# A two-layer sequence model: the norm and a sum of the projection moved between engines, and attention's loads, fills, value copies and averaging rounds put in another order

## The chip, the cores and the metric

The kernel runs on one core of one Trainium2 chip (trn2). The metric is the device time of an execution in microseconds (us). Engines are called by their names: TensorE (PE in the profile, PEld for its weight loads), VectorE (DVE), ScalarE (ACT), GpSimd (POOL) and SyncE (SP), which here only issues transfers.

## The reference, cut to what matters

An input x of 4 batches x 1024 tokens x 256 channels goes through four blocks, each of them x = x + f(layernorm(x)): a state-space layer, a mixture of 8 experts, causal attention with 16 heads of 16 channels and rotated queries and keys, and a mixture of 16 experts with a shared one. The change touches the attention block alone:

```python
Q, K, V = jnp.split(jnp.einsum('bsi,oi->bso', x, W_qkv), 3, axis=-1)
Q, K, V = (to_heads(Q), to_heads(K), to_heads(V))
Q, K = (apply_rope(Q), apply_rope(K))        # x0*cos - x1*sin, x0*sin + x1*cos
scores = jnp.einsum('bhqd,bhkd->bhqk', Q, K) / jnp.sqrt(jnp.float32(d_k))
scores = jnp.where(causal, scores, -jnp.inf)
attn = jax.nn.softmax(scores, axis=-1)
out = jnp.einsum('bhqk,bhkd->bhqd', attn, V)
```

## The kernel before, in words

The program is a chain of phases (front, run_experts, project_qkv, attention, back, run_experts, finish), each in a block of its own: no engine begins a phase before all have ended the one ahead. Inside a phase each engine has its own queue, written out in full and executed in order, and the queues meet only at semaphores. Two phases matter.

**project_qkv** (line 1222) takes the 4096 tokens in 8 groups of 512, four tiles of 128 each. GpSimd gathers the rows of two experts for each token by indirect transfers (line 1337, eight a group). VectorE's add_experts (from line 1373) multiplies them by their weights and adds them to x in two rounds of four instructions (lines 1379 and 1383), then takes mean and variance and writes var_eps (line 1392). GpSimd raises it to the power -1/2 (line 1343), VectorE's normalise writes the normed rows (line 1398, two pointers: mean and factor), TensorE transposes them (line 1479), ScalarE copies the result (line 1441), and TensorE multiplies it by the weights: four products for queries and keys, even and odd channels apart (line 1490), and one for the values (line 1497), which ScalarE copies (line 1448). Rotation is four products of VectorE for queries and four for keys (rotate, line 1406) and then, on GpSimd, a difference and a sum for each (add_turned, lines 1350 and 1351). ScalarE rounds each result (hi, line 1454), VectorE takes what is left (lo, line 1411), and SyncE stores both parts to DRAM, eight transfers a group. The loops run over ticks; in a tick each engine works on different groups:

```python
for tick in range(groups + 2):                     # GpSimd, line 1354
    gather(tick + 1, first half); rsqrt(tick); gather(tick + 1, second half)
    add_turned(tick - 2, 0); add_turned(tick - 2, 1)
```

VectorE's order in a tick is add_experts(tick), four differences of tick - 3, normalise(tick), rotate(tick - 1); ScalarE's is copy_xn(tick), four roundings of tick - 2, copy_v(tick). SyncE stores in its tick the sum x2 of the group, the values of the group before and the queries and keys of the group three back, and waits in that order.

**attention** (line 1508) takes 32 pairs of heads (eight a batch), numbered p. For a pair it needs queries and keys in both parts, spread over partitions 0 to 63 (load, line 1624, eight transfers of 128 KB, each into 16 partitions, all on SyncE's queue), in a ring of four places (RINGQ). Partitions 64 up hold fills: zeros in qs, ones in ks; the row at partition 96 of qs is the negated maximum of each query, which a transfer puts there (row, line 1638). Two passes over the scores follow. In the first, TensorE computes 24 pieces of up to 512 keys (piece, line 1781) and VectorE takes the running maximum of each (line 1724). The pieces go through a ring of four PSUM banks; after the last, TensorE transposes the maxima into the next bank of that same ring (transpose_max, line 1787) and ScalarE negates them (negate, line 1736), which frees the bank. In the second pass TensorE computes the transposed scores in 18 chunks (line 1795) and ScalarE takes their exponentials (line 1743); GpSimd masks the 16 diagonal squares (line 1698). Then TensorE averages the values in ten rounds, four products side by side in each (average, line 1811), the profile counting each of them as two; round 8 and 9 with 128 columns, the others with 256. The values of a batch come in one transfer of 1 MB (load_v, line 1636) and GpSimd copies them to place (values, line 1690, eight copies).

All engines follow one count of steps, 18 a pair (NX): at step 18p + i TensorE issues chunk j of an earlier pair, whose second pass begins LAG = 27 steps after its first (so j = i + 9 modulo 18, of pair p - 2 up to i = 8 and of pair p - 1 from i = 9 on), at i = TURN = 2 the transposed maxima of pair p - 1, then one or two pieces of pair p, and then rounds of the averages, where avg_at names j. ScalarE in a step runs the exponential of that chunk, then at i = 3 negate(p - 1), in this order:

```python
avg_at = {1: (0, 1), 5: (2, 3), 9: (4, 5), 12: (6, 7), 16: (8, 9)}     # line 1587
```

With j = i + 9 the five blocks stand at i = 10, 14, 0, 3 and 7. The piece in slot x waits for the release of what lay four places earlier in the ring (bank_free, line 1766): for x = 5, issued at i = 4, that is the bank of the transposed maxima. The steps i = 0 and 1 issue x = 0 and 1, i = 2 issues x = 2 and 3, i = 3 issues x = 4.

SyncE's loop (line 1652) issues per tick load(tick + 1), load_v at each eighth tick, a store and row(tick - 1); load(p) waits until the chunks of pair p - 4 are done. At the start it issues load(0), load(1), the values, load(2), then row(0), and load(3) ahead of row(1). Four fills come first: GpSimd's zeros (line 1677, 64 x 8192), later and vs (lines 1679 and 1680), VectorE's ones (line 1711, 64 x 8192). TensorE runs keep_busy products (line 1818) meanwhile and waits for all fills; where no chunk is due it runs keep_busy in the chunk's place. At step 72 ScalarE issues the fetch of 4 MB of expert weights (line 2446).

## Time and profile before

| | us |
|---|---|
| median of 3 runs | 1811.72 (1811.04 to 1818.42) |
| the profiled execution | 1815.95 |
| its span in the trace | 1814.2 |
| TensorE busy | 1567.3 (86%) |
| VectorE busy | 1014.3 (56%) |
| ScalarE busy | 707.6 (39%) |
| GpSimd busy | 565.3 (31%) |

The trace is that of the profiled execution, counted from its span's start; project_qkv lies between about 751 and 925 us, attention between 925 and 1440. TensorE's matmuls are pipelined and their ends modelled, so that its rows overlap. A row "x4" joins four instructions: its us is from the first's start to the last's end. What stands in brackets at the end of a row is how long the engine was idle before it and what released it. PEclk is TensorE's granted clock as a share of 2.4 GHz: 0.50 is the lower level, 1.2 GHz.

### The profile page before, as it was taken

To read this page: it belongs to the slowest core of one execution; us is meant where nothing else is said; L and a number is where in the kernel's file an instruction comes from. 1 tells how busy PE (TensorE), PEld (TensorE's weight loads), DVE (VectorE), ACT (ScalarE), POOL (GpSimd) and SP (SyncE) were. 2 spreads that over 40 slices of the span, in tenths; PEclk is the share of its full clock that TensorE was granted. 3 is DMA by queue.
4 is the path that set the end of the run, shared out by engine and by line. 5 is a ranking of instruction groups with operands and counts; after the bars stand their busy time and mean duration, and the time that the engine had idled before them with its cause. 6 is when DMAs were issued, how large, how long until landed. Compare 5 with 4: busy or idle time off the path is not lost. (4 is left out here: it accounts for less than half of the span.)

```text
span 1814.2 us, 29698 instructions
## 1 busy us (share of the span) xinstructions
PE 1567.3 (86%) x9335; PEld 1107.4 (61%) x9335; DVE 1014.3 (56%) x3338; ACT 707.6 (39%) x1487; POOL 565.3 (31%) x993
## 2 busy tenths in 40 slices
PE   0999999982999999588658999999999668399998
PEld 0577777771666666454336666666666456288787
DVE  1245444442222222378858778878888257465556
ACT  0444444430222222122205667767777512154410
POOL 2122333344000000378522232232332238500076
PEclk9899999995999999799779999999999867599999
DMA  8100111112222221358596866666764276445444
GB/s 296 54 24 25 47 47 47 36 53 96 67 65 65 65 66 57 122 177 288 178 199 79 173 108 94 93 102 95 116 91 72 63 228 209 177 153 157 136 134 147
DMA packets 150807, 204.08 MB, mean 112 GB/s; under 512 B 20352, under 2 KB 119168, under 8 KB 150400
## 3 DMA queue, kind: packets, MB, share of 16 engines
q1 hardware_dynamic: 102688, 130.05, 32.1%
q10 hardware_dynamic: 35680, 38.56, 6.2%
q0 software_dynamic: 12288, 33.57, 5.7%
q8 instruction: 80, 1.31, 0.3%
q14 instruction: 71, 0.58, 0.1%
HBM read 116.91 MB, written 84.93 MB: 111 GB/s over the span
## 5 line engine op out<-in xcount | busy, mean ns | idle before, releaser
L1743 ACT ACTIVATE t_probs<-t_ps_st 128x512 f32<-128x512 f32 x576 | 313.7, 596 | 145.5 <-PE t_ps_st L1795 138.5
L1724 DVE CUSTOM_DVE_ANT_0 t_seen<-t_ps_s,t_later 128x512 bf16<-128x512 f32 (+3 forms) x512 | 286.2, 587 | 25.2 <-PE t_ps_s L1781 22.9
L1795 PE MATMUL t_ps_st<-t_qs,t_ks 128*128 128x512 f32 (+3 forms) x768 | 247.0, 371 | 10.0 <-DMA t_qs<-t_neg_max 7.6
L1781 PE MATMUL t_ps_s<-t_ks,t_qs 96*128 96x512 f32 (+3 forms) x768 | 251.9, 369 | 0.5 <-ACT t_neg_max L1736 0.5
L1698 POOL TENSOR_SCALAR_AFFINE_SELECT t_probs<-t_probs 128x128 f32<-128x128 f32 x512 | 136.4, 304 | 297.2 <-ACT t_probs L1743 295.5
L1795 PEld LDWEIGHTS t_ps_st<-t_qs,t_ks 128*128 128x128 f32 x768 | 139.6, 193 | 86.0 <-ACT t_probs L1743 37.8
L1724 DVE CUSTOM_DVE_ANT_0 t_seen<-t_ps_s,t_later,t_first_max 128x512 bf16<-128x512 f32 (+3 forms) x256 | 140.6, 549 | 57.5 <-PE t_ps_s L1781 57.3
L1337 POOL DMA_INDIRECT d_ye<-outputs_dram,r_pos_all x64 | 64.1, 1002 | 326.8 <-POOLq L1099 309.0
L1811 PE MATMUL t_ps_o<-t_probs,t_vs 128*17 128x256 f32 (+1 forms) x2560 | 157.0, 364 | 3.3 <-POOL t_probs L1698 2.8
L1781 PEld LDWEIGHTS t_ps_s<-t_ks,t_qs 96*128 96x128 f32 x768 | 142.5, 195 | 17.2 <-ACT t_neg_max L1736 0.8
L832 PE MATMUL ps_h<-w_in,xnt 128*128 128x512 f32 x256 | 125.5, 615 | 23.1 <-ACT xnt L666 23.1
L1131 PE MATMUL m_ps_h<-w_sb,m_xt 128*128 x284 | 135.5, 600 | 0.0
L1146 PE MATMUL m_ps_y<-w_sb,m_ht 128*128 x568 | 134.2, 379 | 0.0
L1202 ACT ACTIVATE m_xt<-m_ps_x 128x256 f32<-128x256 f32 x150 | 57.5, 383 | 174.5 <-PE m_ps_x L1124 174.5
L1174 DVE TENSOR_TENSOR m_h<-m_ps_h,b_sb 128x512 f32<-128x512 f32 x71 | 49.1, 692 | 131.6 <-PE m_ps_h L1131 129.7
L2223 POOL DMA_INDIRECT f_ye<-outputs_dram,r_pos_all x64 | 62.9, 983 | 170.1 <-POOLq L1099 151.0
L1212 ACT ACTIVATE m_ht<-m_ps_ht 128x128 f32<-128x128 f32 (+1 forms) x150 | 63.9, 426 | 128.2 <-PE m_ps_ht L1139 128.0
L1146 PEld LDWEIGHTS m_ps_y<-w_sb,m_ht 128*128 128x128 f32 x568 | 102.5, 190 | 11.0
L1811 PEld LDWEIGHTS t_ps_o<-t_probs,t_vs 128*17 128x17 f32 x2560 | 59.5, 97 | 75.4 <-issue 27.1
L1124 PE MATMUL m_ps_x<-ident,m_x_t 128*128 128x128 f32 x300 | 58.7, 278 | 41.5 <-DMA m_x_t<-gathered_dram 40.3
L351 POOL TENSOR_TENSOR xi<-xi,sig_z 128x512 f32<-128x512 f32 x32 | 40.6, 1269 | 161.1 <-ACT sig_z L678 160.9
L1185 DVE TENSOR_TENSOR m_y<-m_ps_y,b_sb 128x256 f32<-128x256 f32 x71 | 30.1, 424 | 104.7 <-PE m_ps_y L1146 104.7
(306 smaller groups left out, 2797.9 us busy)
## 6 DMA issues: line engine op xcount, KB each, us to landing
m_x_t<-gathered_dram SPq DMA_DIRECT2D x150, 128.0 KB, 2.1
outputs_dram<-m_y ACTq DMA_DIRECT2D x150, 128.0 KB, 1.7
t_qs<-qkt_dram SPq DMA_DIRECT2D x128, 128.0 KB, 5.8
t_ks<-qkt_dram SPq DMA_DIRECT2D x128, 128.0 KB, 5.9
qkt_dram<-d_hi SPq DMA_DIRECT2D x32, 256.0 KB, 4.1
qkt_dram<-d_lo SPq DMA_DIRECT2D x32, 256.0 KB, 4.1
headst_dram<-t_att SPq DMA_DIRECT2D x32, 256.0 KB, 7.3
x_t<-in_x_dram SPq DMA_DIRECT2D x8, 512.0 KB, 4.4
```

The lines of the kernel that those rows point to most:

```text
L832: last = nc.tensor.matmul(ps_h[h][:], xnt[:, n % 2, j, :], w_in[:, j, h * DI:(h + 1) * DI], start=(j == 0), stop=(j == KD - 1))
L1131: last = nc.tensor.matmul(ps_h[t % 2][:], xt[:, t % 2, j, :], w_up[:, j, bass.ts(expert[t], width)], start=(j == 0), stop=(j == KD - 1))
L1146: last = nc.tensor.matmul(ps_y[t % 2][:], ht[:, t % 2, j, :], w_down[:, j, bass.ts(expert[t], DM)], start=(j == 0), stop=(j == blocks - 1))
L1212: nc.scalar.activation(ht[:, t % 2], ps_ht[t % 2][:], ACT.Relu if relu else ACT.Copy).then_inc(ht_ready, 1)
L1337: nc.gpsimd.indirect_dma_start(out=ye[:, g % 2, j, i, :], out_offset=None, in_=outputs[:, :], in_offset=bass.IndirectOffsetOnAxis(ap=kept[ ...
L1698: nc.gpsimd.affine_select(out=diag, in_=diag, compare_op=ALU.is_ge, fill=0.0, base=0, pattern=[[1, P]], channel_multiplier=-1).then_inc(ma ...
L1724: nc.vector.tensor_tensor_reduce(out=seen[:, (NP * p + x) % (RS + 1), 0:keys], in0=bank_of(p, x)[:, 0:keys], in1=masks, scale=1.0, scalar= ...
L1743: nc.scalar.activation(probs[:, p % 2, i // NST, base:base + STC], ps_st[(NX * p + i) % RT][:], ACT.Exp, scale=HD ** -0.5).then_inc(exp_re ...
L1781: nc.tensor.matmul(bank_of(p, x)[:, 0:keys], qs[0:MAX_ROW, at, qc * P:(qc + 1) * P], ks[0:MAX_ROW, at, k0:k0 + keys], start=True, stop=Tru ...
L1795: last = nc.tensor.matmul(ps_st[(NX * p + i) % RT][:, col:col + width], ks[:, at, kc * P:(kc + 1) * P], qs[:, at, q0:q0 + width], start=Tr ...
L1811: last = nc.tensor.matmul(ps_o[32 * g:32 * g + VR, col:col + width], vs[:, (p // PAIRS) % 2, kc, 2 * (p % PAIRS) + head, :], probs[:, p % ...
L2223: nc.gpsimd.indirect_dma_start(out=ye[:, g % R, j, i, :], out_offset=None, in_=outputs[:, :], in_offset=bass.IndirectOffsetOnAxis(ap=kept[ ...
```

## The change

In project_qkv the norm is written by ScalarE from a bias (-mean times factor), which VectorE computes in a new small instruction (shift); GpSimd's power waits until the norm before it has read its factor. Of the four results of the rotation, the last sum goes from GpSimd to VectorE (last_sum), with a semaphore of its own. ScalarE's order in a tick is normalise(tick), copy_v(tick - 1), copy_xn(tick), the roundings.

In attention the fills are cut by ring place: place 0 first (VectorE fills its ones), the others on GpSimd after the mask table; TensorE waits for three small fills and, at a pair's first piece, for its place. The keys of pair 0 are loaded on ScalarE's queue. SyncE issues load(0), load(1), then row(0), then load(2) and the first values, then load(3) ahead of row(1). The values of a later batch are loaded at tick 4 of the batch before and copied at its tick 5, after that tick's masks. The rounds stand in four blocks: by j = i + 9 at i = 11, 16, 2 and 7.

```diff
+            def shift(g):
                 dve.wait_ge(rstd_ready, g + 1)
-                wait(dve, xnt_done, KD * g)
-                for j in range(J):
-                    nc.vector.tensor_scalar(xn[:, j, :], x2[:, g % 2, j, :], mean_var[:, j, 0:1], rstd[:, j:j + 1],
-                                            ALU.subtract, ALU.mult).then_inc(xn_ready, 1)
+                wait(dve, xn_ready, J * g)
+                nc.vector.scalar_tensor_tensor(out=bias[:], in0=mean_var[:, :, 0], scalar=-1.0, in1=rstd[:], op0=ALU.mult,
+                                               op1=ALU.mult).then_inc(bias_ready, 1)
+
+            def last_sum(g):
+                dve.wait_ge(by_ready, 8 * g + 8)
+                wait(dve, lo_ready, NB * g)
+                nc.vector.tensor_tensor(qk[:, NB - 1, :], by[:, g % 2, 1, 2, :], by[:, g % 2, 1, 3, :], ALU.add).then_inc(last_sum_ready, 1)
...
                 if live(tick):
-                    normalise(tick)
+                    shift(tick)
+                if live(tick - 2):
+                    last_sum(tick - 2)
...
+            def normalise(g):
+                act.wait_ge(bias_ready, g + 1)
+                wait(act, xnt_done, KD * g)
+                for j in range(J):
+                    nc.scalar.activation(xn[:, j, :], x2[:, g % 2, j, :], ACT.Identity, bias=bias[:, j:j + 1],
+                                         scale=rstd[:, j:j + 1]).then_inc(xn_ready, 1)
...
-    avg_at = {1: (0, 1), 5: (2, 3), 9: (4, 5), 12: (6, 7), 16: (8, 9)}
+    avg_at = {2: (0, 1, 2), 7: (3, 4), 11: (5, 6, 7), 16: (8, 9)}
...
             load(0)
-            for tick in range(pairs + 5):
-                if live(tick + 1):
+            load(1)
+            for tick in range(1, pairs + 5):
+                if tick > 1 and live(tick + 1):
                     load(tick + 1)
-                if live(tick) and tick % PAIRS == 0:
-                    load_v(tick // PAIRS)
+                if tick % PAIRS == PAIRS // 2 and live(tick + PAIRS // 2):
+                    load_v(tick // PAIRS + 1)
                 if live(tick - 4):
                     store(tick - 4)
                 if live(tick - 1):
                     row(tick - 1)
+                if tick == 1:
+                    load(2)
+                    load_v(0)
...
-            nc.gpsimd.memset(qs[KS:P].bitcast(FP32), 0.0).then_inc(q_zeroed, 1)
...
+            zero_rows(0)
...
+            for p in range(1, RINGQ):
+                zero_rows(p)
+                nc.gpsimd.memset(ks[KS:P, 2 * p:2 * p + 2].bitcast(FP32), 1.0).then_inc(rows_filled, 1)
...
+                if tick == 0:
+                    values(0)
                 if live(tick - 2):
                     mask(tick - 2)
+                if tick % PAIRS == PAIRS // 2 + 1 and live(tick + PAIRS // 2):
+                    values(tick // PAIRS + 1)
...
-            nc.vector.memset(ks[KS:P].bitcast(FP32), 1.0).then_inc(filled, 1)
+            nc.vector.memset(ks[KS:P, 0:2].bitcast(FP32), 1.0).then_inc(filled, 1)
...
+            for part in range(4):
+                load_rows(act, 0, ks, 1, part, part // 2)
...
-            pe.wait_ge(filled, 5)
-            pe.wait_ge(q_zeroed, 1)
+            pe.wait_ge(filled, 3)
```

## Rows read from the trace of the kernel before

**Rows 1.** Stretches: us, busy time by engine (x count), PEclk, DMA share, GB/s
```profile
1216.69:1231.17 14.48, 14.48 (x137) 9.46 (x133) 12.51 (x49) 10.41 (x21) 4.29 (x16) 1.00 0.67 93
...
952.36:971.48 19.12, 14.69 (x57) 11.75 (x56) 13.84 (x51) 7.60 (x14) 4.73 (x16) 0.82 0.63 73
...
971.48:985.01 13.53, 13.23 (x108) 8.87 (x112) 12.18 (x49) 9.90 (x21) 4.23 (x16) 1.00 0.62 80
...
1062.71:1080.65 17.94, 16.35 (x137) 10.41 (x133) 12.78 (x49) 10.58 (x22) 9.17 (x33) 0.90 0.70 131
...
1182.19:1202.17 19.98, 17.67 (x137) 10.99 (x133) 12.93 (x49) 10.70 (x21) 9.16 (x33) 0.83 0.65 120
...
1303.71:1319.30 15.59, 14.60 (x137) 9.55 (x133) 12.53 (x49) 10.43 (x22) 9.13 (x33) 1.00 0.79 146
...
961.00:967.00 6.00, 6.00 (x17) 5.03 (x18) 4.14 (x15) 3.66 (x7) 0.58 (x2) 0.50 0.49 57
...
925.00:936.80 11.80, 8.14 (x14) 3.49 (x15) 7.45 (x3) 0.00 (x0) 11.49 (x4) 0.79 0.95 118
```

**Rows 2.** Timeline of GpSimd, project phase: start us, us, instruction
```profile
854.12 1.27 POOL L1351 TENSOR_TENSOR d_qk<-d_by 128x512 f32<-128x512 f32 x1
...
860.54 1.22 POOL L1343 TENSOR_TENSOR d_rstd<-d_var_eps,mhalf 128x4 f32<-128x4 f32 x1
```

**Rows 3.** Timeline of VectorE, project phase
```profile
854.15 2.72 DVE L1379 SCALAR_TENSOR_TENSOR d_part<-d_ye,r_prob_all,d_x 128x256 f32<-128x256 f32 x4 [1.66 <-issue]
...
856.79 1.67 DVE L1383 SCALAR_TENSOR_TENSOR d_x<-d_ye,r_prob_all,d_part 128x256 f32<-128x256 f32 x4
...
860.09 0.17 DVE L1392 TENSOR_SCALAR d_var_eps<-d_mean_var 128x4 f32<-128x4 f32 x1
...
876.40 0.17 DVE L1392 TENSOR_SCALAR d_var_eps<-d_mean_var 128x4 f32<-128x4 f32 x1
...
876.48 3.56 DVE L1411 TENSOR_TENSOR d_lo<-d_qk,d_hi 128x512 f32<-128x512 f32 x4
...
879.96 4.21 DVE L1398 TENSOR_SCALAR d_xn<-d_x,d_mean_var,d_rstd 128x256 f32<-128x256 f32 x4
```

**Rows 4.** Instructions of line 2120: duration ns min/median/max, first and last start
```profile
L2120 ACT ACTIVATE k_xn<-whole_sum,k_bias,k_rstd x32: 583/588/601, 1459.1 to 1557.3; 128x256 f32<-128x256 f32 x32
```

**Rows 5.** Timeline of ScalarE, end of the project phase
```profile
900.08 0.60 ACT L1448 ACTIVATE d_v<-d_ps_v 128x512 f32<-128x512 f32 x1 [1.13 <-PE d_ps_v L1497]
```

**Rows 6.** Timeline of TensorE, start of attention
```profile
936.42 0.94 PE L1818 MATMUL t_ps_st<-causal,ident 128*128 128x256 f32 x2 [3.53 <-POOL t_vs L1680]
...
960.86 0.80 PE L1795 MATMUL t_ps_st<-t_qs,t_ks 128*128 128x512 f32 x1 [4.14 <-DMA t_qs<-t_neg_max]
...
974.20 0.45 PE L1795 MATMUL t_ps_st<-t_qs,t_ks 128*128 128x512 f32 x1
```

**Rows 7.** DMA issues at 952.7 and 1055.5: KB each, us to landing
```profile
t_qs<-t_neg_max SPq DMA_DIRECT2D x1, 8.0 KB, 8.1
...
t_v_raw<-v_dram SPq DMA_DIRECT2D x1, 1024.0 KB, 10.8
```

**Rows 8.** Timeline of TensorE, quiet pair, steps i = 3 and 4
```profile
1230.69 1.06 PE L1811 MATMUL t_ps_o<-t_probs,t_vs 128*17 128x256 f32 x16
...
1231.68 0.50 PE L1795 MATMUL t_ps_st<-t_qs,t_ks 128*128 128x512 f32 x1
...
1232.02 0.34 PE L1781 MATMUL t_ps_s<-t_ks,t_qs 96*128 96x384 f32 x1
```

**Rows 9.** Timeline of ScalarE, the same stretch
```profile
1231.17 0.25 ACT L1736 ACTIVATE t_neg_max<-t_ps_s 16x128 fp32r<-16x128 f32 x1
...
1232.21 2.15 ACT L1743 ACTIVATE t_probs<-t_ps_st 128x512 f32<-128x512 f32 x4 [0.79 <-PE t_ps_st L1795]
```

**Rows 10.** Timeline of TensorE's weight loads, pair 2
```profile
970.21 0.19 PEld L1781 LDWEIGHTS t_ps_s<-t_ks,t_qs 96*128 96x128 f32 x1 [0.33 <-DVE t_first_max L1724]
...
971.78 0.19 PEld L1781 LDWEIGHTS t_ps_s<-t_ks,t_qs 96*128 96x128 f32 x1 [0.80 <-ACT t_neg_max L1736]
```

More of the change, by code:

```diff
@@ L1254, in project_qkv @@
     rstd = sb("d_rstd", [P, J])
+    bias = sb("d_bias", [P, J])
     xn = sb("d_xn", [P, J, DM])
@@ L1461, in _ @@
                         round_qk(tick - 2, n)
-                if live(tick):
-                    copy_v(tick)
         @block.tensor
```

66 lines of the change are left out of this document (42 added, 24 removed).

## The prediction, made before the changed kernel ran

> **What bounds the kernel now.** I read the busy time by stage first. In a quiet pair of the attention phase [rows 1], between two negations, TensorE is busy for all 14.48 us at the full 2.4 GHz, VectorE 12.51, ScalarE 10.41, GpSimd 4.29: there TensorE sets the pace, and any wait that is put into its queue lengthens the pair. The same view shows where pairs are longer: 19.12 us for the first, at a mean granted clock of 0.82, and 17.94, 19.98 and 15.59 us where a batch begins.
>
> The project phase is read on GpSimd's and VectorE's rows [rows 2, 3]. One variance follows the other by 16.31 us (860.09, 876.40). The ring behind that: four gathers on GpSimd, their landing, add_experts on VectorE, the power on GpSimd, four gathers. GpSimd has no gap in it: eight gathers, four sums 1.24 us apart (850.42 to 855.39, of which the row is the last), four gathers, the power at 860.54. VectorE's first part of add_experts starts at 854.15 and takes 2.72 us for four, ending at 856.87, that is 1.48 after GpSimd's last sum.
>
> **The change, part by part. Project phase.** (a) One of GpSimd's four sums goes to VectorE: GpSimd's way to the next power is 1.24 us shorter. VectorE's way is not, fully: the gathers end where the sums begin, 850.42, and add_experts starts 3.73 later, when they have landed; its second four, which nothing slows, take 1.67 us (856.79 [rows 3]), so the first four end at 855.82 instead of 856.87 at best. I take 0.9 us a turn, between 0.6 and 1.24, for the five turns that have sums (groups 3 to 7): -4.6 us. (b) The norm goes from VectorE to ScalarE. In most turns this is beside other work. In the last it is on the path: GpSimd's sums run beside VectorE there, the differences take 3.56 us and the norm 4.21 (879.96 to 884.17) [rows 3]. On ScalarE the same form (128x256, two pointers) takes 588 ns [rows 4], four in 2.2 us, starting after the differences at 880.0 and ending at 882.3. After it stands the copy of the values of the group before (1.1 us), which was ahead of it. The moved sum on VectorE is then ahead of the rotation: 0.7 us alone, up to 1.75 beside GpSimd's sums. Gain 2.1 us (bounds 0.5 and 3). The small product for the bias and the added waits (power after norm, product after norm) find their signals given some 10 us earlier: nothing. From the last values (900.08 [rows 5]) SyncE issues 24 transfers and sets the end; that tail is as before, only earlier. Sum: -6.7 us (-9 to -3).
>
> The row is that three instructions with two SBUF inputs or a doubled rate (first part, difference, norm) stretch beside GpSimd's sums [rows 3]. The Trainium skill (SBUF — State Buffer, "Who interferes with whom") says that a VectorE instruction with two SBUF inputs contends with a GpSimd one that reads SBUF; the moved sum is such a one. By it the sum would cost a full GpSimd sum more in the last turn, and the term would be 1 us smaller.
>
> **Start of attention.** Before, TensorE waited until 936.42 for the fills [rows 6]; the phase starts at 925. The fills by ring place free it at about 929, but the first megabyte of queries and keys moved at 118 GB/s with the queues already at a busy share of 0.95 [rows 1], so it needs 8.9 us after some 2 of latency: 936.3. Gain 0.4 us. Bounds: nothing, and 3.5 us (keep_busy ends at 932.9) if keys on ScalarE's queue doubled the rate.
>
> The Trainium skill (SBUF — State Buffer, "Can I just issue two DMAs to hit both halves?") gives +6% for two transfers at once; by it the gain would be 0.9 us. No run here shows it yet.
>
> Then the queue of SyncE. Before, the row of pair 0 stood behind load(1), the values and load(2) and took 8.1 us to land [rows 7]; TensorE idled 4.14 us before the first chunk [rows 6] and then ran 6 us at 1.2 GHz (granted 0.50) [rows 1]. After, that row goes out alone: both are gone. But load(2), the values and load(3) are now issued behind it, from 952.9 on. A load takes 11 us from its first issue (8.9 and 2) and 8.9 behind another, the values land some 3.6 after the load ahead of them (10.8 from their own issue [rows 7], 7.2 of it behind the load): 963.9, 967.5, 976.4. TensorE is at the first chunk at 956.3 (960.86 - 4.14 - 0.4) and nine steps on, at VectorE's 12.51 / 18 = 0.7 us, it wants load(2) for pair 2: 962.6, so it waits to 964. The row of pair 1 is issued three steps later, some 966.5, **behind load(3)**, and lands at 976.5; six steps after its issue, at 971, it is needed. So chunk (1, 0), at 974.20 before [rows 6], comes at 976.5: 2.3 us later; and a wait of 5 us is followed by 6 us at half clock as the first one was, 3 us more. Start in all: +5.3 us by the third negation (-7 to +8: the lower end is both old losses gone and no new one).
>
> **Beginning of a batch.** The three cost 3.46 + 5.50 + 1.11 = 10.1 us over 14.48 [rows 1], from the row behind load and values, the masks behind the value copies on GpSimd, and the clock after both. The masks' part goes: in mid-batch the copies (2.8 us) stand between two pairs' masks. The row's part moves along to pairs 3, 11 and 19, since load_v still stands behind a load and ahead of a row. At pair 3 it meets the 4 MB of weights that ScalarE fetches at step 72; I give it 4 us there and 0.5 at each of the others. Term: -5.0 us (-9 to -1).
>
> **Blocks of averages.** Around a block TensorE holds the next chunk for 0.34 us (1231.68 to 1232.02) instead of 0.24, and the piece ahead of the block loses as much: 0.2 us a block [rows 8]. One fewer in 31 pairs: -6.2 us. But what stood in the removed places matters. The ring has four banks for the pieces, and the transposed maxima take one; the piece at i = 4 (x = 5) reuses it and waits for negate. ScalarE runs negate after the exponential of chunk i = 3. Before, a block stood at i = 3 between the two: negate ran from 1231.17 to 1231.42 [rows 9], the piece came at 1232.02 [rows 8], 0.6 us to spare. After, the block (three rounds) is at i = 2, ahead of chunk i = 3. From that chunk's start: 0.50 for the chunk [rows 8], 0.03, 0.53 for the exponential (2.15 for four [rows 9]), 0.25, 0.05 make 1.36 us; TensorE gets to the piece after 0.34 + 0.12 + 0.24 = 0.70. **A new wait of 0.66 us in 29 pairs** (3 to 31): +19.1 us. The trace has one pair without a block there, pair 2: its weight load waited 0.80 us for that negation (971.78), and the one before waited 0.33 for the maximum that frees a bank (970.21) [rows 10]. For this second wait, and one for the last maximum (the block at i = 0 covered both; now it is at i = 16), I take 0.25 us a pair, between nothing and 0.37: +7.3 us. Term: +20.2 us (+10 to +24).
>
> **Sum:** -6.7 + 5.3 - 5.0 + 20.2 = +13.8 us. The profiled execution took 1815.95 us (span 1814.2), 4.2 above the median of the three runs, 1811.72; so 1829.8 for such an execution and **1825.5 us** for the median. A measurement of this kernel can tell about 0.5% (9 us) from no change.
>
> **Rivals.** (A) The new wait is not paid. If negate came in time, or TensorE had room that its modelled ends hide, the blocks give -6.2 alone: -6.7 + 5.3 - 5.0 - 6.2 = -12.6, 1799 us, faster. For it: no wait of TensorE is recorded in quiet pairs. Against it: pair 2, and 14.48 of 14.48 busy. It decides where ScalarE's negation ends less than 0.70 us after chunk i = 3 starts; an exponential and the negation alone are 0.78. (B) The loads at the start drain in time: if load(3) lands before 971 no row waits, the start is -7 instead of +5.3, and the whole is +1.5: 1813 us. It needs 3.1 MB in the 16 us to 971, near 200 GB/s; the rows give 118 for query and key loads, and 146 where values are among them (1303.71 [rows 1]). (C) The three waits within 2 us let the clock fall in each pair: 14.48 us has then some 3 us at half rate, +1.5 us in 29 pairs, 1869 us. Against it: the 13.53 us after pair 2's waits were granted 1.00 [rows 1].
>
> **How the numbers follow.** My forecast has 0.55 (0.48 of it above +9 us), A 0.20, B 0.17, C 0.08. Slower by over 0.5%: 0.48 + 0.08 = 0.56; within: 0.07 + 0.17 = 0.24; faster: 0.20. The likeliest case alone spans 1817 to 1836 (its terms' ends, seldom all together). The range goes down to 1797, which takes in most of A, and up to 1836; C and the tail of A are left out.
>
> **What would show it.** Each step right: variances 15.4 us apart in the project phase and the last value copy some 6.7 us earlier; first chunk without a wait; a wait of some 5 us at chunk (1, 0) named by the transfer of the negated maxima; no masks awaited at a batch's beginning; quiet pairs of 15.1 to 15.2 us, with TensorE waiting for t_neg_max at line 1781's matmul in nearly every pair. Quiet pairs of 14.3 us would make A right and the forecast wrong; a third negation before 978 (by the old phase's start) would make B right.

## The result, and the profile after

The changed kernel takes 1827.44 us (median of 7 runs, 1824.85 to 1829.17), the kernel before 1812.86 on the same chip (median of 7, 1809.52 to 1819.13): a ratio of 1.0079, with a 95% interval of 1.0063 to 1.0094. It is 14.6 us slower; 1825.5 us was forecast. The profiled execution has a span of 1825.5 us against 1814.2, 11.3 more.

How the 11.3 us come about can be read from marks in the two traces: the first variance of the project phase, SyncE's first load of the attention phase, the third negation, and the last negation (pair 31).

| from ... to ... | before | after | difference |
|---|---|---|---|
| start, first variance (nothing changed there) | 768.4 | 766.3 | -2.1 |
| first variance, first load of attention | 156.7 | 148.3 | -8.4 |
| first load, third negation | 59.9 | 67.2 | +7.3 |
| third negation, last negation | 435.4 | 448.5 | +13.1 |
| last negation, end | 393.8 | 395.1 | +1.3 |

The project phase gave more than forecast, the start of attention took more, and the long middle of attention lost what the blocks of averages cost, less what the beginnings of batches gave.

**Project phase.** VectorE's and then ScalarE's timeline of the changed kernel:

```profile
766.31 0.17 DVE L1396 TENSOR_SCALAR d_var_eps<-d_mean_var 128x4 f32<-128x4 f32 x1
...
869.69 0.17 DVE L1396 TENSOR_SCALAR d_var_eps<-d_mean_var 128x4 f32<-128x4 f32 x1
...
873.25 1.22 DVE L1401 SCALAR_TENSOR_TENSOR d_bias<-d_mean_var,d_rstd 128x4 f32<-128x4 f32 x1
874.40 0.68 DVE L1407 TENSOR_TENSOR d_qk<-d_by 128x512 f32<-128x512 f32 x1
```

```profile
874.51 2.07 ACT L1453 ACTIVATE d_xn<-d_x,d_bias,d_rstd 128x256 f32<-128x256 f32 x4 [8.34 <-DVE d_bias L1401]
...
889.82 0.60 ACT L1467 ACTIVATE d_v<-d_ps_v 128x512 f32<-128x512 f32 x1 [1.13 <-PE d_ps_v L1521]
```

The eight variances span 103.38 us (766.31 to 869.69); before it was 107.98 (768.42 to 876.40). In the late turns one follows the other by 15.17 to 15.29 us, where it was 16.31. From the last variance to the last copy of values it is 20.13 us, and was 23.68 [rows 3, 5]. The bias, a 128x4 instruction, takes 1.22 us in the last turn, since GpSimd's sums run beside it; in the turn before it takes 0.15. Even so the norm is done at 876.58, 6.89 us after the variance, where it was 7.77.

**Quiet pairs.** The stretches between negations in the changed kernel (columns as in [rows 1]); 958.81 to 981.83 is pair 2, the line below it the 6 us behind its wait, 1095.28 to 1110.50 a quiet pair, the last two are pairs 12 and 20, in which the values of the next batch travel:

```profile
942.71:958.81 16.10, 13.84 (x57) 10.10 (x56) 13.49 (x53) 7.45 (x14) 0.37 (x2) 0.89 0.93 150
958.81:981.83 23.02, 16.38 (x114) 10.54 (x113) 12.97 (x52) 9.93 (x20) 8.89 (x33) 0.85 0.70 79
967.96:973.96 6.00, 6.00 (x35) 3.68 (x36) 2.49 (x9) 2.09 (x4) 0.29 (x1) 0.63 1.03 117
981.83:1001.54 19.71, 15.24 (x129) 10.07 (x129) 12.39 (x49) 10.14 (x22) 4.34 (x16) 0.95 0.83 171
1001.54:1019.17 17.63, 17.16 (x130) 11.26 (x129) 12.76 (x50) 10.48 (x21) 4.38 (x16) 0.86 1.08 249
1095.28:1110.50 15.22, 14.73 (x129) 9.72 (x129) 12.48 (x50) 10.23 (x21) 4.34 (x16) 1.00 0.64 88
1125.72:1141.70 15.98, 14.95 (x129) 9.72 (x129) 12.57 (x50) 10.29 (x21) 4.34 (x16) 1.00 0.74 129
1248.35:1263.68 15.33, 14.83 (x129) 9.74 (x129) 12.49 (x50) 10.29 (x22) 4.34 (x16) 1.00 0.78 138
```

A quiet pair now takes 15.22 us, of which TensorE is busy for 14.73, at a granted clock of 1.00. Before, 14.48 of 14.48 were busy [rows 1]. The waits of TensorE between 920 and 1460 us (total, times, longest) name what is new:

```profile
PE t_ps_s L1827 <- ACT t_neg_max L1778: 13.7, 30, 0.5
PE t_ps_st L1841 <- DMA t_qs<-t_neg_max: 6.8, 2, 6.3
PE t_ps_s L1827 <- DMA t_ks<-qkt_dram: 6.6, 2, 4.4
PE t_ps_st L1841 <- ACT t_probs L1785: 5.3, 6, 4.1
PE t_ps_o L1857 <- issue: 0.5, 1, 0.5
```

The first line is a wait for the negation in 30 pairs; before there was one such wait. Masks, which had held TensorE three times at the beginnings of batches, are no longer in the list. The wait itself, in TensorE's timeline of a quiet pair:

```profile
1094.26 0.50 PE L1841 MATMUL t_ps_st<-t_qs,t_ks 128*128 128x512 f32 x1
1094.59 0.28 PE L1827 MATMUL t_ps_s<-t_ks,t_qs 96*128 96x256 f32 x1
1094.71 0.39 PE L1841 MATMUL t_ps_st<-t_qs,t_ks 128*128 128x512 f32 x1
1095.59 0.45 PE L1827 MATMUL t_ps_s<-t_ks,t_qs 96*128 96x384 f32 x1 [0.48 <-ACT t_neg_max L1778]
```

and in ScalarE's:

```profile
1094.79 0.60 ACT L1785 ACTIVATE t_probs<-t_ps_st 128x512 f32<-128x512 f32 x1 [1.99 <-PE t_ps_st L1841]
1095.28 0.25 ACT L1778 ACTIVATE t_neg_max<-t_ps_s 16x128 fp32r<-16x128 f32 x1
```

The chunk of i = 3 starts at 1094.26, its exponential at 1094.79, the negation behind it at 1095.28, and the piece that needs the bank at 1095.59. That is 1.33 us after the chunk's start; the forecast had worked out 1.36 from parts. TensorE's gap is 0.48 us.

**Start of attention.** TensorE's waits there, and how long the row of pair 1 took to land:

```profile
926.44 0.79 PE L1827 MATMUL t_ps_s<-t_ks,t_qs 96*128 96x512 f32 x1 [4.39 <-DMA t_ks<-qkt_dram]
955.13 0.59 PE L1827 MATMUL t_ps_s<-t_ks,t_qs 96*128 96x512 f32 x1 [2.21 <-DMA t_ks<-qkt_dram]
...
967.96 0.79 PE L1841 MATMUL t_ps_st<-t_qs,t_ks 128*128 128x512 f32 x1 [6.26 <-DMA t_qs<-t_neg_max]
```

```profile
t_qs<-t_neg_max SPq DMA_DIRECT2D x1, 8.0 KB, 8.8
```

The row of pair 0, issued at 943.06 on an empty queue, landed in 2.3 us, and chunk (0, 0) did not wait. The row of pair 1, issued at 959.14 behind the loads of pairs 2 and 3 and the values, took 8.8 us; chunk (1, 0) waited 6.26 us for it, and the 6 us after that had a granted clock of 0.63. Pair 3 then lost time in a way that the forecast had not spelled out. ScalarE's timeline, then TensorE's:

```profile
992.35 7.17 ACTq L2491 DMA_DIRECT2D wgu_sb<-in_w_gu_dram  x2
...
999.56 2.08 ACT L1785 ACTIVATE t_probs<-t_ps_st 128x512 f32<-128x512 f32 x4 [6.62 <-issue]
```

```profile
1000.21 0.80 PE L1841 MATMUL t_ps_st<-t_qs,t_ks 128*128 128x512 f32 x1 [4.14 <-ACT t_probs L1785]
```

ScalarE needed 7.17 us to issue two transfers of 2 MB each, its exponentials stood behind them, and TensorE waited 4.14 us for an exponential. In the kernel before the same two issues cost ScalarE 3.58 us and TensorE 1.65.

### The profile page after: what moved, and what is told of

The parts are those of the page before. It is cut to its first block and busy times, and to the rows that moved or that the text cites. A ratio compares the mean times of both kernels' runs of the same rounds, so it can differ in the third digit from the quotient of the medians.

```text
span 1825.5 us, 29737 instructions
## 1 busy us (share of the span) xinstructions
PE 1573.9 (86%) x9335; PEld 1118.3 (61%) x9335; DVE 998.3 (55%) x3322; ACT 714.3 (39%) x1519; POOL 563.8 (31%) x991
## 5 line engine op out<-in xcount | busy, mean ns | idle before, releaser
L1766 DVE CUSTOM_DVE_ANT_0 t_seen<-t_ps_s,t_later 128x512 bf16<-128x512 f32 (+3 forms) x512 | 290.5, 587 | 86.2 <-PE t_ps_s L1827 84.2
L1827 PE MATMUL t_ps_s<-t_ks,t_qs 96*128 96x512 f32 (+3 forms) x768 | 261.6, 375 | 20.8 <-ACT t_neg_max L1778 13.7
L1841 PE MATMUL t_ps_st<-t_qs,t_ks 128*128 128x512 f32 (+3 forms) x768 | 242.1, 366 | 12.3 <-DMA t_qs<-t_neg_max 6.8
L1857 PE MATMUL t_ps_o<-t_probs,t_vs 128*17 128x256 f32 (+1 forms) x2560 | 149.9, 362 | 0.5 <-issue 0.5
```

Source lines behind the costliest of these rows:

```text
L1766: nc.vector.tensor_tensor_reduce(out=seen[:, (NP * p + x) % (RS + 1), 0:keys], in0=bank_of(p, x)[:, 0:keys], in1=masks, scale=1.0, scalar= ...
L1827: nc.tensor.matmul(bank_of(p, x)[:, 0:keys], qs[0:MAX_ROW, at, qc * P:(qc + 1) * P], ks[0:MAX_ROW, at, k0:k0 + keys], start=True, stop=Tru ...
L1841: last = nc.tensor.matmul(ps_st[(NX * p + i) % RT][:, col:col + width], ks[:, at, kc * P:(kc + 1) * P], qs[:, at, q0:q0 + width], start=Tr ...
L1857: last = nc.tensor.matmul(ps_o[32 * g:32 * g + VR, col:col + width], vs[:, (p // PAIRS) % 2, kc, 2 * (p % PAIRS) + head, :], probs[:, p % ...
```

## The experiments

Twelve kernels ran, in four groups, each group on one chip. Ratios are to the kernel before on that chip (its median was 1841.77 us in the first group, 1812.86, 1813.72 and 1814.38 in the others), so it is the ratios that are compared from group to group. On the chip of the first group the extra time lies behind attention: from the last negation to the end a1_old_blocks takes 422.4 us, the changed kernel on the other chip 395.1. The table also gives, from each profile, the time from SyncE's first load to the third negation and to the last one, and a quiet pair. Each profile is of one execution, which can lie some us beside its kernel's median (8 us below it for a2_before_new_blocks, 4 above it for d3_old_order).

| kernel | ratio, 95% interval | to 3rd negation | to last | quiet pair |
|---|---|---|---|---|
| before | 1 | 59.9 | 495.3 | 14.48 |
| changed | 1.0079 [1.0063, 1.0094] | 67.2 | 515.8 | 15.22 |
| a1_old_blocks | 0.9969 [0.9949, 0.9989] | 64.1 | 493.8 | 14.49 |
| a2_before_new_blocks | 1.0097 [1.0059, 1.0134] | 57.3 | 505.1 | 15.22 |
| a3_negate_first | 0.9993 [0.9970, 1.0016] | 64.4 | 494.7 | 14.49 |
| a4_row_first | 1.0055 [1.0031, 1.0078] | 62.2 | 512.7 | 15.23 |
| b3_blocks_0_3 | 0.9959 [0.9944, 0.9973] | 66.3 | 492.7 | 14.29 |
| c1_fetch_later | 1.0066 [1.0046, 1.0086] | 67.1 | 513.8 | 15.23 |
| c2_project_alone | 0.9947 [0.9932, 0.9962] | 58.4 | 494.5 | 14.49 |
| c3_keys_on_sync | 1.0097 [1.0076, 1.0119] | 65.2 | 514.2 | 15.23 |
| d1_blocks_row | 0.9920 [0.9895, 0.9945] | 59.2 | 484.2 | 14.29 |
| d3_old_order | 0.9899 [0.9877, 0.9921] | 56.6 | 484.3 | 14.29 |
| e1_old_order_fetch | 0.9905 [0.9881, 0.9928] | 54.7 | 480.4 | 14.29 |
| f1_values_behind_row | 0.9909 [0.9888, 0.9929] | 54.5 | 477.2 | 14.29 |

### The blocks of averages

**The old blocks in the changed kernel.**

```diff
-    avg_at = {2: (0, 1, 2), 7: (3, 4), 11: (5, 6, 7), 16: (8, 9)}
+    avg_at = {1: (0, 1), 5: (2, 3), 9: (4, 5), 12: (6, 7), 16: (8, 9)}
```

> The changed kernel with the five old blocks of averages (at steps 10, 14, 0, 3 and 7 of a pair). Theory (the removed blocks had covered TensorE's waits for the maxima and the negation): the quiet pair comes back from 15.22 to about 14.48 us, no wait of TensorE for t_neg_max at line 1827's matmul is left beyond pair 2, and the kernel is some 20 us faster than the changed one, 1807 us, a ratio of 0.996 to the kernel before. Rival A (the blocks' places don't matter, each block costs 0.2 us): one block more in 31 pairs makes it 6 us slower than the changed kernel, 1834 us. If part of the slower pair comes from the other edits (order on ScalarE's or GpSimd's queue), the pair stays above 14.6 us.

Measured: a ratio of 0.9969, 0.0110 below the changed kernel's 1.0079, which is 20 us of 1812.86 (the two intervals together leave about 15 to 25). A quiet pair:

```profile
1072.43:1086.94 14.51, 14.51 (x137) 9.48 (x133) 12.51 (x49) 10.45 (x21) 4.30 (x16) 1.00 0.67 93
```

TensorE is busy throughout again. Rival A, by which it would have been slower, is out.

**The new blocks in the kernel before.** The edit of a1_old_blocks the other way round, in the kernel before.

> The kernel before with the four new blocks alone. Theory: quiet pair 15.2 us against 14.48, TensorE's waits for t_neg_max in nearly every pair, and 20 to 23 us slower than the kernel before: ratio 1.011 to 1.013. Rival A: 6 us faster, ratio 0.997. If the new places only hurt together with the other edits, the ratio is between the two.

```profile
1106.57:1121.76 15.19, 14.71 (x129) 9.71 (x129) 12.47 (x50) 10.22 (x21) 4.34 (x16) 1.00 0.63 88
```

```profile
PE t_ps_s L1781 <- ACT t_neg_max L1736: 14.4, 30, 0.6
...
PE t_ps_o L1811 <- POOL t_probs L1698: 0.9, 2, 0.6
```

The pair is 15.22 us and the wait is there 30 times: the blocks alone make it, with none of the other edits. But the ratio is 1.0097 where 1.011 to 1.013 was expected (the interval reaches both), and in the trace the attention phase is only 9.8 us longer than before, not 21. The losses at the beginnings of batches shrank: pairs 8, 9, 16 and 24 take 15.88, 15.55, 16.65 and 15.72 us, 2.9 over the quiet 15.22 together, where the kernel before lost 10.1 (and c2_project_alone, with the same attention, 11.0). In the traces, then, the parts of this change don't add: beside the new blocks the move of the values is worth some 2 us, beside the old ones 8. That a slower pair gives the masks and rows the slack that they lacked is a reading that was not tried by itself. Nor do the times show it: the profiled execution was the fastest of four, 8.3 us below their median, and the ratio stands for 18 us (11 to 25 by its interval), not for the trace's 9.8.

**The negation ahead of the exponential.**

```diff
-                if live(q):
-                    exponentials(q, j)
                 if i == 3 and live(p - 1):
                     negate(p - 1)
+                if live(q):
+                    exponentials(q, j)
```

> The changed kernel, with ScalarE's negation put ahead of the exponential of the same step. It touches one of the two waits alone: the piece that reuses the bank of the transposed maxima. Theory: this wait is the 0.66 us a pair of the forecast; the negation comes 0.5 us sooner, TensorE's wait for t_neg_max goes, and the kernel is 12 to 19 us faster than the changed one (1808 to 1815 us), the quiet pair 14.6 to 14.8 us; the waits for t_row_max and t_first_max, 0.2 to 0.3 us a pair, stay. Rival: TensorE's pace in these pairs is set by the waits for the maxima alone (they only move); then it is within 4 us of the changed kernel, with the pair still at 15.2. A second rival: the negation now waits on ScalarE for the maximum, and the exponential behind it comes late; then the pair is longer than 15.2.

```profile
1091.13:1105.62 14.49, 14.48 (x130) 9.75 (x129) 12.46 (x49) 10.01 (x21) 4.37 (x16) 1.00 0.65 93
```

Ratio 0.9993, some 16 us faster than the changed kernel. The quiet pair fell by the whole 0.73 us, more than expected, with the four blocks where they were. The wait is one of order on ScalarE's queue: an exponential of 0.6 us ahead of a negation of 0.25 that TensorE wants sooner.

**Four blocks that cover both waits.** Blocks at i = 11, 0, 3 and 7.

```diff
-    avg_at = {2: (0, 1, 2), 7: (3, 4), 11: (5, 6, 7), 16: (8, 9)}
+    avg_at = {2: (0, 1, 2), 9: (3, 4), 12: (5, 6, 7), 16: (8, 9)}
```

> The changed kernel, still with four blocks of averages, but at steps 11, 0, 3 and 7 of a pair: blocks stand again in the two places that had covered the waits (the last maximum, and the negation). Theory: no wait is left and there is one block less than before, so the quiet pair falls below the 14.48 us of the kernel before, to about 14.28 us; 25 to 29 us faster than the changed kernel, ratio to the kernel before 0.992 to 0.994. Rival: a block costs nothing by itself and the pair with all waits covered is 14.48 us, as it was with five blocks and with the negation put first; then it is 22 us faster than the changed kernel, ratio 0.996. Second rival: a block of three rounds at step 0 or 3 keeps the banks so long that another wait shows; pair above 14.6 us.

```profile
1077.88:1092.22 14.34, 14.34 (x137) 9.69 (x133) 12.42 (x49) 10.15 (x21) 4.25 (x16) 1.00 0.69 94
```

Most pairs take 14.29 us (this one 14.34). Against a1_old_blocks (14.49, five blocks, all covered) that is 0.20 us for one block; against a3_negate_first (14.49, four blocks, the negation mended, the last maximum uncovered) it is 0.20 us for the other wait. That wait shows on TensorE's weight loads in a3_negate_first, in every pair, and nowhere in b3_blocks_0_3:

```profile
1104.81 0.09 PEld L1833 LDWEIGHTS t_ps_s<-ident,t_row_max 128*16 128x16 f32 x1 [0.18 <-DVE t_row_max L1766]
...
1105.36 0.19 PEld L1827 LDWEIGHTS t_ps_s<-t_ks,t_qs 96*128 96x128 f32 x1 [0.33 <-DVE t_first_max L1766]
```

So the 0.73 us of the change are +0.73 for the negation, +0.20 for the maximum, -0.20 for the block less. The ratio, 0.9959, is a little above the 0.992 to 0.994 expected: 22 us faster than the changed kernel, not 25 to 29. Its third negation comes as late as in the changed kernel, and pair 12, where the values travel, now takes 17.96 us against 14.29: with a shorter pair its row is late again (see the last experiment).

### The start of attention

**The row of pair 1 ahead of the load of pair 3.**

```diff
+                if tick == 2:
+                    row(1)
                 if tick > 1 and live(tick + 1):
                     load(tick + 1)
...
-                if live(tick - 1):
+                if live(tick - 1) and tick != 2:
                     row(tick - 1)
```

> The changed kernel, with the row of pair 1 issued ahead of the load of pair 3 on SyncE's queue. Theory (the row lands behind the load's data): TensorE's wait of 6.26 us at chunk (1, 0) falls to under 1 us, the stretch after it is no longer at a lowered granted clock, and the kernel is 6 to 9 us faster than the changed one. The load of pair 3 is issued some 11 us later and must not be late: it is needed near 976 us. Rival: the row waits for the loads already in flight (pair 2 and the values), whatever stands behind it; then the wait stays at 5 us or more and the time is the changed kernel's. Second rival: the loss moves to pair 3 (its load or the weights that ScalarE fetches there): wait at chunk (1, 0) gone, time gained under 3 us.

The waits of TensorE between 955 and 996 us that are left:

```profile
955.40 0.50 PE L1829 MATMUL t_ps_s<-t_ks,t_qs 96*128 96x512 f32 x1 [2.21 <-DMA t_ks<-qkt_dram]
...
971.15 0.50 PE L1829 MATMUL t_ps_s<-t_ks,t_qs 96*128 96x512 f32 x1 [1.29 <-DMA t_ks<-qkt_dram]
...
995.44 0.79 PE L1843 MATMUL t_ps_st<-t_qs,t_ks 128*128 128x512 f32 x1 [4.20 <-ACT t_probs L1787]
```

The row lands in 1.8 us, the wait of 6.26 us at chunk (1, 0) is gone, and the third negation comes 5.1 us earlier. But 2 us are given back by the fifth: the load of pair 3, now behind the row, is 1.29 us late, and the wait for ScalarE's blocked queue is followed by a longer stretch at half clock. Over the 8.5 us behind that wait the granted clock is 0.50 (995.44 to 1003.94), where it is 0.62 in the changed kernel (1000.20 to 1008.70). Six of these us:

```profile
996.77:1002.77 6.00, 5.81 (x32) 4.49 (x31) 3.06 (x12) 3.62 (x8) 1.38 (x5) 0.50 1.09 346
```

The ratio is 0.0024 below the changed kernel's, 4 us; the two intervals overlap, so that the times alone would not show the gain. The trace does: 3.1 us over the phase.

**The keys of pair 0 back on SyncE's queue.**

```diff
-                    if p > 0:
-                        load_rows(sp, p, ks, 1, part, part // 2)
+                    load_rows(sp, p, ks, 1, part, part // 2)
...
-            for part in range(4):
-                load_rows(act, 0, ks, 1, part, part // 2)
```

> The changed kernel with the keys of pair 0 issued by SyncE again, not by ScalarE. Theory (the first megabyte is limited by its transfer, at 117 GB/s with the queues full): TensorE's first piece comes 11.8 us after the phase's start as with two queues, and the time is within 2 us of the changed kernel. Rival: two queues did bring something that the other fills hid; then the first piece is 1 us or more later. Second rival: the load of pair 1 no longer overtakes the keys of pair 0, so that the first piece comes earlier.

The ratio is 1.0097, with an interval that overlaps the changed kernel's: no difference that can be told, and if one, against this kernel. In the trace the first piece comes 11.06 us after the first load, not 11.83. But over the ten kernels that load with two queues it comes 10.95 to 11.83 us after (10.95 in a1_old_blocks, 11.21 in f1_values_behind_row). So one execution with one queue doesn't tell which is sooner, and the second queue brought TensorE nothing that shows.

**SyncE's old order at the start, with the mended blocks.** In b3_blocks_0_3:

```diff
             load(0)
-            load(1)
-            for tick in range(1, pairs + 5):
-                if tick > 1 and live(tick + 1):
+            for tick in range(pairs + 5):
+                if live(tick + 1):
                     load(tick + 1)
+                if tick == 0:
+                    load_v(0)
...
-                if tick == 1:
-                    load(2)
-                    load_v(0)
```

> The changed kernel with blocks at steps 11, 0, 3 and 7, and SyncE's order at the start as in the kernel before (load of pair 1, values, load of pair 2, then row 0, load of pair 3, row 1); the values of later batches stay in mid-batch. Theory: the new order at the start is a loss in itself, since it moves two megabytes of loads from before row 0 to behind it, and the queues have nothing to do before it. The third negation comes 57 to 60 us after the phase's start, as in the kernel before, not 66 to 67; ratio 0.991 to 0.993, some 5 us faster than with the mended blocks alone. Rival: the row of pair 0 now stands behind the loads and lands late again (4 us, and 3 of lowered clock), so that the kernel is no faster than with the blocks alone, ratio 0.996.

Ratio 0.9899 against 0.9959, 11 us faster than with the mended blocks alone, and the third negation comes 56.6 us after the phase's start, not 66.3. The new order of the loads was a loss in itself: its gain on row 0 (2.3 us to land, not 8.1 [rows 7]) is smaller than what it costs to hold back two megabytes of loads until the queue is wanted for the next row. The rival's wait for row 0 came back in part: 2.72 us at chunk (0, 0) in this execution, none in the two later kernels with the same start (e1_old_order_fetch and f1_values_behind_row, where that row took 3.9 and 3.0 us to land).

**Both mendings, with the new order.** The diffs of b3_blocks_0_3 and a4_row_first together.

> The changed kernel with both mendings: blocks at steps 11, 0, 3 and 7, and the row of pair 1 issued ahead of the load of pair 3. Theory (the two losses are in different pairs and add): ratio 0.9959 of the blocks alone, less the 0.0024 that the row's place gave, makes 0.9935. In the trace the third negation comes some 62 us after the phase's start (67.2 in the changed kernel) and half of the 5 us is lost again at pairs 3 and 4. Rival: with shorter pairs nothing of the row's gain is left by pair 5, because the transfers of the start, 4 MB of weights among them, set the time; ratio 0.996.

Ratio 0.9920, 7 us below b3_blocks_0_3; the phase is 8.4 us shorter (484.22 against 492.65), where the row's place alone gave 3.1 in the changed kernel. The third negation comes at 59.2, sooner than the 62 expected, and pairs 3 and 4 give nothing back (36.2 us against 36.1). The rival is out. So of the 9.8 us by which the old order is ahead at the third negation, moving one row gives back 7.1. This kernel and d3_old_order are equal over the attention phase; whether the 0.0021 between their ratios is real can't be told, since their intervals overlap.

### The fetch and the values

**The fetch of weights in pair 6**, in the changed kernel.

```diff
-                if step == 4 * NX:
+                if step == 6 * NX + 9:
                     fetch(act)
```

> The changed kernel, with the two fetches of weights on ScalarE's queue (4 MB) issued at step 117 (in pair 6) and not at step 72 (pair 4). Theory: ScalarE's 6.62 us of issue come from a transfer queue that is full at that time (load of pair 5, values and stores stand there too), and TensorE's 4.14 us for t_probs follow from it; later, with the values out of the way, the issue takes 3.6 us or less and TensorE waits under 2 us: 2 to 5 us faster than the changed kernel, with pairs 3 and 4 together below 33 us instead of 37.3. Rival: the issue of 4 MB takes 6.6 us wherever it stands; the loss moves to pair 6 unchanged, time within 1.5 us.

Pairs 3 and 4 come down to 15.22 us each. The two issues now take ScalarE 2.86 us (1030.80 to 1033.66) and not 7.17, and no wait of TensorE for an exponential is over 0.3 us. But the 4 MB still have to travel. TensorE's wait and the stretch behind it, in pair 7:

```profile
1049.71 0.50 PE L1841 MATMUL t_ps_st<-t_qs,t_ks 128*128 128x512 f32 x1 [2.76 <-DMA t_qs<-t_neg_max]
```

```profile
1043.35:1050.00 6.65, 3.59 (x31) 2.78 (x32) 3.76 (x16) 3.50 (x8) 1.89 (x7) 1.00 1.07 307
1050.00:1056.00 6.00, 6.00 (x39) 3.42 (x39) 3.06 (x11) 2.61 (x6) 0.29 (x1) 0.72 1.12 204
```

Now a row stands behind the weights, and the pair takes 19.77 us. Of 6.9 us at pairs 3 and 4, 5.2 are lost at pairs 6 and 7. The ratio is 1.0066, 2 us better, which the intervals can't tell from nothing. The same edit in d3_old_order:

> The same as the one before, and the fetch of weights at step 117. Theory: pair 3 or 4 no longer waits for ScalarE's blocked queue; the 4 MB take transfer time from one pair later on, 4.5 us there against 6.9 at pairs 3 and 4: 2 us faster than without, ratio 0.990 to 0.992. Rival: with the old order the loads of the start have drained by pair 4 (the kernel before lost 5.2 us at pairs 3 to 5), and the later fetch gains nothing, within 1 us.

Ratio 0.9905 against 0.9899: no difference. The phase is 3.9 us shorter in the trace (480.4 against 484.3), the whole is not measurably so. And the 3.9 are not the fetch's: pairs 3 and 4 take 6.8 us less than in d3_old_order, pairs 6 and 7 6.5 more; the rest is the first pairs and pair 12, which the fetch doesn't touch.

**The project phase alone**, in the kernel before (the functions of that phase from the changed kernel, nothing else):

> The kernel before with the project phase of the changed one alone (the sum on VectorE, the norm on ScalarE). Theory: the whole gain of that phase reaches the end: 6.7 us by the forecast, 8.2 by the two traces, so a ratio of 0.995 to 0.996. Rival: the phase is shorter but the attention phase that follows starts with transfers still under way and loses part of it: 0.998. Quiet pairs of 14.48 us.

Ratio 0.9947, 9.6 us faster (interval 6.9 to 12.3). The whole gain of the phase reaches the end; the attention phase behind it takes 494.5 us, as before. The rival is out.

**The values of mid-batch behind the row.** In d3_old_order the pair with the values takes 19.67 us. Its window, TensorE's wait in it, and the landing of that row:

```profile
1112.52:1132.19 19.67, 17.43 (x137) 11.06 (x133) 12.68 (x49) 10.40 (x21) 4.27 (x16) 0.83 0.69 131
```

```profile
1119.24 0.80 PE L1839 MATMUL t_ps_st<-t_qs,t_ks 128*128 128x512 f32 x1 [2.23 <-DMA t_qs<-t_neg_max]
```

```profile
t_qs<-t_neg_max SPq DMA_DIRECT2D x1, 8.0 KB, 6.4
```

```diff
-                if tick % PAIRS == PAIRS // 2 and live(tick + PAIRS // 2):
-                    load_v(tick // PAIRS + 1)
                 if live(tick - 4):
                     store(tick - 4)
                 if live(tick - 1):
                     row(tick - 1)
+                if tick % PAIRS == PAIRS // 2 and live(tick + PAIRS // 2):
+                    load_v(tick // PAIRS + 1)
```

> The kernel with mended blocks and the old order at the start, and in mid-batch the values issued behind the row of tick 4, not ahead of it (the load of the next pair is issued some 3.5 us later). In the run without this, pair 12 takes 19.67 us against 14.29: a wait of 2.23 us for the row, which took twice as long to land as in a quiet pair, and a granted clock of 0.83 after it; pairs 4 and 20 have smaller losses. Theory (the row lands late because one megabyte of values is ahead of it): pairs 12 and 20 come down to 14.3 to 15 us, 5 us less in all, ratio 0.987. Rival: the load of the next pair meets the values and lands late, so that the loss moves one pair on; ratio 0.990 as without it.

```profile
1105.85:1120.13 14.28, 14.28 (x137) 9.67 (x133) 12.39 (x49) 10.11 (x21) 4.25 (x16) 1.00 0.88 163
1002.24:1019.99 17.75, 16.09 (x137) 10.05 (x133) 12.49 (x49) 10.18 (x22) 6.96 (x24) 0.90 0.75 113
```

Pair 12 is quiet, as is pair 20 (14.29): the row had been late because a megabyte of values was ahead of it. But pair 5 (the second line) takes 17.75 us, where it took 14.40 in d3_old_order. In this execution the values issued at 987.29, behind the weights (979.24), took 13.1 us to land, and the row of pair 4, issued at 1002.51, took 5.8; TensorE waited 1.66 us for it. For that batch the loss moved one pair on, as the rival says, though by the row and not by the load. Those were the values of the second batch; the ones of the third and fourth, at pairs 12 and 20, meet no weights. The phase is 7.1 us shorter (477.2 against 484.3), but the ratio is 0.9909 against 0.9899: the theory holds for its pairs and fails in its time. Whether the 7 us exist outside the profiled execution stays open; the first pairs of attention differ by some us from one execution to the next (the kernel before and c2_project_alone run the same attention phase, and their first chunk waited 4.14 and 3.02 us), and this profiled execution lies 5.7 us below its kernel's median, that of d3_old_order 3.9 above.

The best kernels of the study are d3_old_order, e1_old_order_fetch, f1_values_behind_row and d1_blocks_row, at 0.990 to 0.992 of the kernel before (15 to 18 us faster, and faster than both kernels of the comparison). Nothing measured here tells the four apart.

## Why the prediction was right

The forecast was +13.8 us, the measurement +14.6 between medians and +11.3 between the two profiled spans, to which the measured column below adds up within 0.1. It came out by its main term, which has the right mechanism and size. The other terms each missed by 1.7 to 2.5 us, with signs that cancel; that the total is within 1 us of the medians is luck. The last row of the table lies in stretches that the change doesn't touch, so it is a difference between two executions.

| step | forecast | measured | from |
|---|---|---|---|
| project phase | -6.7 | -8.4 | the two traces; -9.6 by c2_project_alone |
| start, to the third negation | +5.3 | +7.3 | the two traces |
| beginnings of batches, pairs 3 to 5 | -5.0 | -7.5 | -9.2 and +1.7, below |
| blocks | +20.2 | +20.6 | what is left of the middle's +13.1 without the row above; 20 by a1_old_blocks |
| rest | 0 | +1.3 and -2.1 | behind attention, and ahead of the project phase |

**Project phase.** The turns gave 4.60 us (103.38 against 107.98), where 4.6 was forecast, but not as forecast. The step "I take 0.9 us a turn" was too small: in the late turns GpSimd waits for no other engine after the change either, and they are shorter by 1.0 to 1.1 us (15.17 to 15.29 against 16.31), nearly the 1.24 of the sum that it gave away; the five turns with sums gave 5.2. The third variance came 0.64 us later after the second than before (14.16 against 13.52), which the forecast had at nothing, and that brought the sum back to 4.60. The last turn gave 3.55 us, not 2.1. The norm ended only 0.9 us sooner after its variance than before; TensorE began its products for queries and keys 0.9 us sooner after the norm (1.59 against 2.45), and 1.8 us came from these products, which took 8.16 us and not 9.97. The windows of the kernel before and of the changed one over them show the clock at which they ran:

```profile
886.60:896.60 10.00, 9.98 (x17) 4.40 (x18) 8.31 (x12) 1.66 (x4) 5.68 (x4) 0.71 0.31 99
```

```profile
878.20:886.30 8.10, 8.10 (x17) 3.72 (x18) 8.00 (x11) 2.39 (x5) 4.91 (x3) 0.87 0.95 299
```

The forecast had left the clock out there. It had weighed a rule of the Trainium skill (SBUF — State Buffer, "Who interferes with whom") by which the moved sum, with two SBUF inputs beside GpSimd's sums, would make the term 1 us smaller. The trace agrees that the two contend, and either side can pay: in the last turn that sum took 0.68 us beside a sum of GpSimd's, which stretched to 1.80 us against 1.28 alone; in the two ticks after it, the same sum of VectorE's took 1.57 and 1.56 us beside GpSimd's. The term was larger than forecast all the same, not smaller.

**Start.** Waits were where they had been put: none at chunk (0, 0), 2.21 us for the load of pair 2 (about 1.5 forecast), 6.26 us at chunk (1, 0) for a row that stood behind the load of pair 3 (5 forecast), and a lowered clock after it. The row was wanted at 961.7 and came at 968; a4_row_first shows that the queue's order did it, since the row then lands in 1.8 us. What was missed is the first piece, which came 11.83 us after the phase's start, where it had been 11.71, and not 0.4 earlier; the first negation came 0.8 us later, which is within what executions differ by (26.5 to 28.6 us after the first load). The transfers of keys on ScalarE's queue bought nothing that shows: with one queue (c3_keys_on_sync) that piece comes at 11.06, with two at 10.95 to 11.83, the queues being at a busy share of 0.96 in c3_keys_on_sync and in the changed kernel. By the Trainium skill (SBUF — State Buffer, "Can I just issue two DMAs to hit both halves?") two transfers at once would have brought some 6%; of the 8.9 us of transfer that is an estimated 0.5 us, less than the 0.9 between these executions, so that no run here shows it. The term as a whole is more than a chance of one execution: the third negation comes 64.1 to 67.2 us after the first load in the six kernels that start as the changed one (65.7 in the mean; c3_keys_on_sync, with its keys on SyncE, is among them), and 57.3 to 59.9 in the three that start as the one before (58.5), 7.2 apart.

**Beginnings of batches.** The kernel before lost 10.1 us there. After, pairs 12 and 20 lost 0.76 and 0.11, and the masks are gone from the list of waits: -9.2 us. The forecast had taken 1.0 for those two pairs, which is near. The step that was mis-sized is "I give it 4 us there" at pair 3: pairs 3 to 5 took 52.57 us against 48.65, of which three times 0.73 is the blocks', so 1.7 us is what was added there, on top of the fetch's cost in the kernel before. And the mechanism was only half right: the loss came less from a row behind the weights than from exponentials behind ScalarE's own issue of them (6.62 us, and TensorE's 4.14).

**Blocks.** The wait of 0.66 us was forecast as the time from the chunk's start to the end of the negation, less the time that TensorE needs to get there. It measured 0.73 (the pair with the negation first is that much shorter), the second wait 0.20 where 0.25 was taken, and a block 0.20 as forecast: +0.73 a pair in sum, where 0.71 was forecast. That the profile's list gives only 0.46 us for each of the 30 waits is no contradiction; the pace of pairs is the measure, and the weight load ahead of the matmul waits as well, 0.80 us for the negation.

**The rivals.** A (the wait isn't paid) is out by the pair of 15.22 us and by a1_old_blocks. B (the loads at the start drain in time) is out by the wait of 6.26 us; the third negation came 67.2 us after the first load, where B wanted less than 53. C (the clock falls in each pair) is out: quiet pairs were granted 1.00.

What the forecast did not see is that its terms can depend on each other. By the traces, moving the values was worth 8 us with the old blocks and some 2 with the new ones (a2_before_new_blocks against the changed kernel), and when the pairs became shorter than before, at 14.29 us, the mid-batch row was late once more, 2.23 us and a lowered clock. The sum did not suffer from it: it sets the full loss of the kernel before against the small one of the changed kernel, and those two are what the traces show.

## What to carry to other kernels

Before work is removed from a place or moved in a queue, ask what stood behind it in time: a block of matmuls that seems to cost 0.2 us may be what covers a wait of 0.7, and then the cheap mend is on the other engine's queue (a short instruction that others wait for goes ahead of a long one) or in choosing which block to drop. A small transfer on which a chunk depends landed in 1.8 to 2.9 us on an empty queue, in 6.1 to 6.4 us when issued 6.8 us after a megabyte of values (the row of pair 11 in b3_blocks_0_3, d1_blocks_row and d3_old_order; 3.8 when issued 8.6 us after, in the changed kernel), and in 8.4 to 10.5 us behind two loads and the values, so the order of issue at a start is worth as much as the arithmetic; but large loads that are held back for it must travel later, and meet the next small one. Parts of a change should be measured with the others in place, since slack made by one hides or shows the cost of another.

## What was not expected of the hardware

- Issuing a transfer can block the engine that issues it, by an amount that depends on what else is in flight: the same two transfers of 2 MB took ScalarE 7.17 us to issue in the changed kernel, 4.14 in the kernel before (995.57 to 999.71), and 2.86 at a calmer time (c1_fetch_later). ScalarE's exponentials stood behind them.
- With two queues the first transfers arrived no sooner than with one, as far as the executions tell: 10.95 to 11.83 us in ten kernels against 11.06 in one (117 GB/s in the changed kernel, 122 in c3_keys_on_sync).
- What a wait of TensorE costs is more than its length: behind the waits of 6.26 us (changed kernel) and 2.76 us (c1_fetch_later) the next 6 us had a granted clock of 0.63 and 0.72, and pair 12 of d3_old_order, with a wait of 2.23 us, took 5.4 us more than a quiet pair at a clock of 0.83. The waits of 0.48 us in every pair of the changed kernel went with a clock of 1.00.
